# Weight-check loads one output tile earlier, weight casts and copies spread over block 0, in a fused FFN kernel

## The reference, cut to what matters

```
tf    = sigmoid(sum(cond))                          # one number per batch
decay = exp(-exp(w)) * (0.5 + 0.5*tf)
ek, ekv = exp(min(k,30)), exp(min(k,30))*v
nf, df  = forward scans   a = a*decay + ekv (ek)    # along the 1024 steps
nb, db  = the same scans run backward
num = nf + nb - ekv + exp(min(u+k,30))*v            # den likewise
m   = sigmoid(r) * num/max(den,1e-8) * (0.8+0.2*tf)
h   = m @ W1.T            # 1024 -> 4096
q   = clip(round(h/0.1), 16-bit range)
out = x + gelu(q*0.1) @ W2.T                        # 4096 -> 1024
```

## Time and profile before

| | us |
|---|---|
| median of 3 timed runs | 1911.16 (1910.56 to 1913.1) |
| profiled execution, its own time | 1906.45 |
| its span | 1904.6 |
| PE busy | 1723.3 (90%) |
| DVE busy | 1281.7 (67%) |
| ACT busy | 1046.7 (55%) |
| PE waited for `mo` at the starts of blocks (L505) | 59.6 in 7 waits |
| PE waited for the residual addition (L561, L505) | 9.4 + 1.5 |
| block 0's hidden stage, from its third step | 132.25 to 238.6 |

### The profile page before, as it was taken

The page is one execution under the profiler, slowest core; times in us unless marked ns, Lnnn a source line. Parts: engine busy times, 40 slices in busy tenths (PEclk is TensorE's granted clock), DMA queues, the critical chain, the costliest instruction groups (busy, mean ns, idle before and its releaser), DMA issues.

```text
span 1904.6 us, 27493 instructions
## 1 busy us (share of the span) xinstructions
PE 1723.3 (90%) x10882; PEld 1076.1 (57%) x10882; DVE 1281.7 (67%) x2040; ACT 1046.7 (55%) x1422; POOL 24.7 (1%) x44
## 2 busy tenths in 40 slices
PE   1367989899998999899998999989998999989998
PEld 0123434487446864388545874478544884468643
DVE  8964987679586766678685775768776774933211
ACT  5544853488336863388444873378544883345400
POOL 0040000000000000000000000000000000000000
PEclk9678999899998999999998999989998999999999
DMA  8499866465454645456454654556454554545442
GB/s 215 116 238 334 299 204 182 144 198 191 148 168 143 188 150 177 144 181 213 139 174 136 199 170 142 171 169 194 153 183 132 178 189 148 157 132 161 142 146 73
DMA packets 119990, 329.55 MB, mean 173 GB/s; under 512 B 13232, under 2 KB 21424, under 8 KB 119344
## 3 DMA queue, kind: packets, MB, share of 16 engines
q1 hardware_dynamic: 117168, 304.67, 50.5%
q0 software_dynamic: 2688, 23.07, 5.1%
HBM read 319.30 MB, written 48.23 MB: 193 GB/s over the span
## 4 chain that ended last, share of the span: by engine, by line
PE 79%; DMA 3%; DVE 3%; ACT 1%; issue 1%; SPq 0%; DVEq 0%
PE ps L561 42%; PE ps L505 37%; DMA chk_full<-in_w_dram 3%; DVE chk_full L1107 1%; ACT chk_i L758 1%; DVE a L1039 0%; ACT mo L695 0%; DVE a L1041 0%; DVE a L1043 0%; DVE xy L1099 0%; SPq L303 0%; SPq L317 0%; DVE mo L1049 0%; SPq L318 0%; ACT q L699 0%
## 5 line engine op out<-in xcount | busy, mean ns | idle before, releaser
L561 PE MATMUL ps<-act,w_ring 128*128 128x512 f16 x4096 | 890.1, 379 | 9.4 <-DVE xy L1099 9.4
L505 PE MATMUL ps<-mo,w_ring 128*128 128x256 f16 x6272 | 704.4, 276 | 61.2 <-DVE mo L1049 59.6
L505 PEld LDWEIGHTS ps<-mo,w_ring 128*128 128x128 f16 x6272 | 620.5, 99 | 146.7 <-DVE mo L1049 61.6
L561 PEld LDWEIGHTS ps<-act,w_ring 128*128 128x128 f16 x4096 | 400.6, 98 | 490.9 <-issue 15.5
L758 ACT ACTIVATE chk_i<-chk_full 128x1024 int8<-128x1024 f32 x64 | 67.5, 1054 | 440.3 <-DMA chk_full<-in_w_dram 440.3
L1107 DVE SCALAR_TENSOR_TENSOR chk_full<-chk_i,chk_full 128x1024 f32<-128x1024 int8 x64 | 78.3, 1223 | 252.5 <-ACT chk_i L758 252.3
L1092 DVE SCALAR_TENSOR_TENSOR act<-a,act 128x1024 f16<-128x1024 f32 x128 | 156.2, 1220 | 132.3 <-ACT act L751 132.3
L745 ACT ACTIVATE a<-q 128x1024 f32<-128x1024 int16 x128 | 135.3, 1057 | 31.4 <-DVE act L1092 27.2
L751 ACT ACTIVATE act<-a 128x1024 f16<-128x1024 f32 x128 | 134.2, 1049 | 0.9
L482 PE MATMUL ps<-mo,w_ring 128*128 128x512 f16 x128 | 45.1, 532 | 87.3 <-DVE mo L1032 87.3
L495 PE MATMUL ps<-mo,w_ring 128*128 128x512 f16 x384 | 90.0, 399 | 16.5 <-ACT q L699 12.5
(11 more groups left out here) (95 smaller groups left out, 1454.2 us busy)
## 6 DMA issues: line engine op xcount, KB each, us to landing
w_ring<-w1s SPq DMA_DIRECT2D x168, 512.0 KB, 3.7
w_ring<-w_half SPq DMA_DIRECT2D x144, 512.0 KB, 4.2
chk_full<-in_w_dram SPq DMA_DIRECT2D x64, 512.0 KB, 5.2
V<-in_fside_dram SPq DMA_DIRECT2D x64, 256.0 KB, 4.5
R<-in_x_dram SPq DMA_DIRECT2D x64, 256.0 KB, 4.6
w_half<-in_w_dram POOLq DMA_DIRECT2D x16, 1024.0 KB, 14.5
xy<-in_x_dram SPq DMA_DIRECT2D x64, 256.0 KB, 2.6
out_dram<-xy SPq DMA_DIRECT2D x64, 256.0 KB, 4.4
```

The source lines that it names most:

```text
L505: mm = pe.matmul(dst[:, f, :], wp_ring[:, k, r, f, q, :], mo[:, op, q, p, :], start=(fresh and f == 0 and q == 0 and p == 0), stop=(q == K ...
L561: mm = pe.matmul(y_ps[y][:, :], w2_ring[:, k, f, :], act[:, a, p, :], start=(a == 0 and p == 0), stop=(a == FT - 1 and p == 1))
```

## The change

- `load_check` moves forward by one output tile: the load of piece `8n + d + 1` now stands where that of piece `8n + d` stood, and the last of a block stands in the row of tile 6. The second piece's load goes ahead of the ring load for tile 1's second half, and the third piece's load comes right behind that ring load.
- On ACT and DVE each piece's conversion and comparison go behind the work for the next block that followed them (`operands_hi`, `tile_group`, `operand_sums`, `operands_lo`, `part`), and the comparison behind the residual addition, except the first and the last piece's.
- The W2 casts get waits on POOL: on the seventh mixing tile, on block 0's hidden steps and on its first output halves. The copies of W1's quadrants wait for block 0's output halves. SP's ring loads wait for the one cast that they need, and the first of block 1 for the copies, which now have a semaphore each.

No arithmetic is added or taken away.

```diff
                 if i < 2 * STEPS:
                     sp.wait_ge(s_w1cast[i // 2], 16)
-                if i == 2 * STEPS:
-                    for d in range(DT):
-                        sp.wait_ge(s_w2cast[d], 16)
+                if 2 * STEPS <= i < 2 * STEPS + 4:
+                    sp.wait_ge(s_w2cast[i % 2], 16)
+                if 2 * STEPS + 4 <= i < 2 * STEPS + 2 * DT:
+                    sp.wait_ge(s_w2cast[(i - 2 * STEPS) // 2], 16)
...
-                for _ in range(3 if n == 0 else 5):
+                for _ in range(2 if n == 0 else 4):
                     ring_load()
                 load_check(DT * n + 1)
+                ring_load()
+                load_check(DT * n + 2)
                 for d in range(2, DT):
...
-                    load_check(DT * n + d)
+                    if d < DT - 1:
+                        load_check(DT * n + d + 1)
...
             for d in range(DT):
+                if d == 0:
+                    pool.wait_ge(s_out, CT - 1)
+                elif d == 1:
+                    pool.wait_ge(s_h0, 2 * FPS)
+                elif d < 6:
+                    pool.wait_ge(s_h0, FPS * (d + 3))
+                else:
+                    pool.wait_ge(s_y, d - 5)
                 pool.dma_start(w2_half[d], w2_full[d]).then_inc(s_w2cast[d], 16)
             for s in range(STEPS):
+                pool.wait_ge(s_y, 3 + s // 2)
...
@@ DVE, the end of an output stage
-                check(at + 6)
+                check(at + 5)
                 if nxt:
                     operand_sums(n + 1, 2)
                     operands_lo(n + 1, 2)
+                    divide(g0 + 7)
                 residual_sum(n, 6)
-                if nxt:
-                    divide(g0 + 7)
-                check(at + 7)
+                check(at + 6)
                 if nxt:
                     operand_sums(n + 1, 3)
                     operands_lo(n + 1, 3)
+                check(at + 7)
                 residual_sum(n, 7)
```

More of the change, by code:

```diff
@@ L147, in adaln_ffn_kernel @@
         s_w2cast = [sem(f"s_w2cast{k}") for k in range(DT)]
-        s_w1copy = sem("s_w1copy")
+        s_w1copy = [sem(f"s_w1copy{k}") for k in range(STEPS)]
         s_wsumin = [sem(f"s_wsumin{k}") for k in range(2)]
@@ L292, in ring_load @@
                     sp.wait_ge(s_w1cast[i // 2], 16)
-                if i == 2 * STEPS:
-                    for d in range(DT):
-                        sp.wait_ge(s_w2cast[d], 16)
+                if 2 * STEPS <= i < 2 * STEPS + 4:
+                    sp.wait_ge(s_w2cast[i % 2], 16)
+                if 2 * STEPS + 4 <= i < 2 * STEPS + 2 * DT:
+                    sp.wait_ge(s_w2cast[(i - 2 * STEPS) // 2], 16)
                 if i == 2 * STEPS + 2 * DT:
-                    sp.wait_ge(s_w1copy, 16 * 3 * STEPS)
                     for k in range(2):
                         sp.wait_ge(s_wstore[k], 16 * STEPS)
+                    for t in range(STEPS):
+                        sp.wait_ge(s_w1copy[t], 16 * 3)
                 if i >= RING:
@@ L454, in _ @@
             for d in range(DT):
+                if d == 0:
[6 more added lines that the diff above has]
+                    pool.wait_ge(s_y, d - 5)
                 pool.dma_start(w2_half[d], w2_full[d]).then_inc(s_w2cast[d], 16)
             for s in range(STEPS):
+                pool.wait_ge(s_y, 3 + s // 2)
                 pool.wait_ge(s_w1cast[s], 16)
                 for r, h, k in ((WP1, 0, 0), (WP2, 0, 1), (WP4, 1, 1)):
-                    pool.dma_start(w1s[s][:, r, :, :], w1_quads[s][:, h, :, k, :]).then_inc(s_w1copy, 16)
+                    pool.dma_start(w1s[s][:, r, :, :], w1_quads[s][:, h, :, k, :]).then_inc(s_w1copy[s], 16)
             for d in range(DT):
                 pool.wait_ge(s_w2cast[d], 16)
-            pool.wait_ge(s_w1copy, 16 * 3 * STEPS)
+            for s in range(STEPS):
+                pool.wait_ge(s_w1copy[s], 16 * 3)
         @block.tensor
@@ L820, in _ @@
                     hidden_block(n, nxt, g0)
+                if nxt:
+                    operands_hi(n + 1, 0)
                 check_i8(at)
                 if nxt:
-                    operands_hi(n + 1, 0)
+                    tile_group(g0 + 5)
                 check_i8(at + 1)
                 if nxt:
-                    tile_group(g0 + 5)
+                    operands_hi(n + 1, 1)
                 check_i8(at + 2)
                 if nxt:
-                    operands_hi(n + 1, 1)
+                    tile_group(g0 + 6)
                 check_i8(at + 3)
                 if nxt:
-                    tile_group(g0 + 6)
+                    tile_group(g0 + 7)
                 check_i8(at + 4)
-                if nxt:
-                    tile_group(g0 + 7)
                 check_i8(at + 5)
-                check_i8(at + 6)
                 if nxt:
@@ L840, in _ @@
                     reciprocal(g0 + 7)
-                check_i8(at + 7)
+                check_i8(at + 6)
                 if nxt:
                     operands_hi(n + 1, 3)
+                check_i8(at + 7)
             def general_block(m):
@@ L1176, in _ @@
                     hidden_block(n, nxt, g0)
-                check(at)
                 if nxt:
@@ L1180, in _ @@
                     operands_lo(n + 1, 0)
+                check(at)
                 residual_sum(n, 0)
-                check(at + 1)
+                if nxt:
+                    part(3, g0 + 4)
                 residual_sum(n, 1)
                 if nxt:
-                    part(3, g0 + 4)
                     part(0, g0 + 5)
-                check(at + 2)
+                check(at + 1)
                 if nxt:
@@ L1190, in _ @@
                     operands_lo(n + 1, 1)
+                    part(1, g0 + 5)
                 residual_sum(n, 2)
+                check(at + 2)
                 if nxt:
-                    part(1, g0 + 5)
                     part(2, g0 + 5)
                     part(3, g0 + 5)
-                check(at + 3)
                 residual_sum(n, 3)
@@ L1199, in _ @@
                     part(0, g0 + 6)
+                check(at + 3)
+                if nxt:
                     part(1, g0 + 6)
                     part(2, g0 + 6)
-                check(at + 4)
                 residual_sum(n, 4)
@@ L1206, in _ @@
                     part(0, g0 + 7)
+                check(at + 4)
+                if nxt:
                     part(1, g0 + 7)
-                check(at + 5)
                 residual_sum(n, 5)
```

## The result

| | before | after |
|---|---|---|
| median of the timed runs | 1911.55 (1910.56 to 1913.1, 4 runs) | 1857.6 (1856.04 to 1862.72, 4 runs) |
| ratio, with its 95% interval | 1 | 0.9722 (0.9702 to 0.9742) |
| profiled execution, its span | 1906.45, 1904.6 | 1856.92, 1854.3 |
| PE, DVE, ACT busy | 1723.3, 1281.7, 1046.7 | 1710.3, 1282.2, 1044.0 |
| PE's waits at the starts of blocks 1 to 7 | 61.1 | 28.6 |

The change makes the kernel 54 us faster, 2.8%. I had forecast 1810 with a range up to 1838; the time lies 20 us above the range. The direction was right, and half of the gain was missing.

A forecast was written before the change was run, and what follows sets the result against it. PE, busy 90%, was taken as the bound, standing still at block starts and in block 0. 1906.45 - 78.0 - 3.7 - 30.5 + 11.2 = 1805.5; with 4.7 carried over, 1810, range 1796 to 1838.

The forecast's parts named there:

- Starts, the wait removed: Starts of blocks 1 to 7: PE's wait for `mo`, its clock loss and a residual wait go, 78.0 us gained.
- Starts, the new wait: Starts of blocks 1 to 7: PE newly waits 1.6 us each for ACT's `seed`, 11.2 us lost, without clock loss.
- the store takes 4.2 until the next issue: SP's queue at block 2's end: 4.2 us from a store to the next issue, one link of the check's loop.
- My second rival: Block starts: check 6 ends 2 to 4 us later, a longer wait and clock loss add 41 us, 1851; chance 0.12.
- the first three: Cases the range was to hold: the forecast (0.50), no new wait at starts (0.20), part of the wait kept (0.12).
- Waits for the residual in blocks 1 to 7: Output stage outside block 0: PE's waits for the residual go with the late check, 3.7 us gained.
- Block 0: Block 0 from its third hidden step: all waiting and its clock loss go, 30.5 us, 23 of it in the hidden stage.
- nothing in DVE's row is later than PE needs it: End of block 0's hidden stage: DVE needs about 23 us until the first residual addition, PE wants it after 27.7.
- My third rival: Block 0: five casts delay weight-sum loads, so the hidden stage keeps its 23 us, 1833; chance 0.12.
- The offset of 4.7 us: Whole kernel: the timed median lay 4.7 us above the profiled execution, carried over from 1805.5 to 1810.
- The slow rival: Output tiles: SP's loop sets the pace, decisive from about 18.1 us a tile; 1971 at 19.4; chance 0.04.
- The signs that I had named: Profile after: `mo` waits near 0, `seed` waits 1 to 2 us, no clock fall, block 0 in 194 to 198 us.

The follow-up runs named there:

- experiments 5: The changed kernel with two check buffers, the int8 piece placed on a part of `q16`: 1816.63 us, ratio 0.9507.
- 11: The changed kernel with two check buffers, one W2 cast per hidden step, and two pieces of DVE's work in block 0 moved earlier: 1798.98 us, ratio 0.9429.
- Experiment 8: The changed kernel, still one check buffer, with check loads for pieces 3 to 7 issued behind the next tile's store and residual load: 1823.89 us, ratio 0.9552.
- Experiment 4: The changed kernel with each block's last check piece converted behind the next block's second spill and compared behind its second seed: 1857.42 us, ratio 0.9715.
- 9: The changed kernel with two check buffers, but casts and copies as in the kernel before: 1824.75 us, ratio 0.9554.
- experiment 1: The kernel before with only block 0's part of the change (casts and copies spread), the check as before: 1908.4 us, ratio 0.9982.
- experiment 2: The changed kernel with casts and copies as in the kernel before, so the check's part alone: 1862.49 us, ratio 0.9745.

## Why the prediction was right or wrong

*Starts, the wait removed (78.0 us).* Right as a step: the eight microseconds behind the last comparison are gone, and experiments 5 and 11 show runs of 848 matmuls without a gap. What failed is the next term.

*Starts, the new wait (11.2 us).* This term measured 38.1. The mechanism that I gave it is there in the rows, in the order I gave. Four things were off. The first: "the store takes 4.2 until the next issue" is the size that failed: it measured 5.62 to 5.75 at block 2's end and 5.3 to 5.8 over blocks 1 to 6, with the check's load just ahead of the store, where the change itself puts it in time, and I took the price from a place where it wasn't (and from the shortest of six there, 4.2 to 4.6). Experiment 8 moves it away again, and the link is back at 4.4. That is 1.5 us at each start, and my margin on the operand pair was 0.4, so PE waits for `mo` again. The second: "Behind `seed`, DVE's next need is at 807.7 at the earliest and is met" forgot the last residual load, whose addition stands in DVE's row ahead of it and which waits for the store behind the last check load. Experiment 4 shows that mending the forecast wait alone brings nothing. The third: "no clock loss" cost 5.6 us. The fourth: one block's end was taken for all seven, and the addition of tile 6, which has 2.8 us to spare in my working, came late at four of them (6.8 us of the waits).

My second rival, "block starts keep a real part of the wait", is the one that came in kind: check 6 ends 1.4 to 4.2 us later than I had it (it said 2 to 4), and the clock falls at three starts. It had put that down to some tenths on each link, and one link had 1.5 of it. It had 52 us for the starts (the 11.2 and 41 more), so the 38.1 lie between it and the forecast, nearer to it. It had a chance of 0.12 and should have had a far larger one, since the sum stood or fell with a margin of 0.4 us at the end of a chain of some ten links. And the range was set against its own words: it was said to take in "the first three in full", but the second rival's 1851 lies outside its upper end of 1838.

*Waits for the residual in blocks 1 to 7 (3.7 us), and what was costed at nothing.* Right: no wait of PE at L576 is left outside block 0, DVE's and ACT's busy time is the same, and no wait of PE stands behind the copies of W1's quadrants, though beside them a store of SP's took 7.1 us until the next issue (275.63 to 282.75).

*Block 0 (30.5 us).* Its hidden stage is right to the microsecond: 83.04 us for 384 matmuls, as 6 x 13.86. The step that failed is "nothing in DVE's row is later than PE needs it". I had put two sentences side by side that don't go together: five casts in the hidden stage, which leaves three for the output stage, 6.9 us apart; and DVE's budget of "about 23 us until the first residual addition", worked out as if loads came at once. It took 49 us (215.2 to 264.3). "One cast is in flight at a time", at "about 5 us", failed as well: the three took 9.7 to 10.6 us each, so they overlapped. The last weight sums' loads fall right among them. The waits of 12.2 and 8.2 us follow, and some 4.5 of clock. Experiments 5 and 9 between them give the part's value with the loop out of the way, 6.7 us; with the other check (experiment 1) it was 1.9, with the changed kernel's (against experiment 2) 4.9. From experiment 5 to 11 the edits of casts and order give 17.7, so these two together are most of the cause; which has how much of it in that kernel I haven't separated.

My third rival had placed the casts' harm in the hidden stage, where there was none. That its size, 23 us, is close to what the output stage lost is luck. The Trainium skill, DMA: Bandwidth & Descriptors, section "Queues, rings and completion order", has each engine take turns between queues packet by packet; the rows of 225 to 235 us don't show one for one as the earlier trace rows did, since SP's queue moved 1053 packets beside the casts' 67, so they neither bear it out nor refute it. I had used it for that rival only, and not asked which loads a cast would meet in the output stage.

*The offset of 4.7 us* between the profiled and the timed execution did not come back: 1857.6 against 1856.92, 0.7. It was carried over on one pair of numbers, and made the forecast higher, so it didn't cause the miss.

*The slow rival*, SP's loop setting the pace of all tiles, was close in kind. From the comparison's end at 750.5 to the next at 769.2 are 18.7 us, over the 18.1 from which I said that it decides. But the next is 11.1 (769.2 to 780.3), so the loop doesn't go on at that pace, and it costs at the block's end alone.

*The signs that I had named.* V's first load in block 0 landed within 6 us (4.2), and block 0's hidden stage has no wait for the quantisation or the ring. Against it: six of the seven starts wait over 3 us in all, the clock falls at three, and the third hidden step to the end of block 0's outputs took 218.8 us and not 194 to 198.

## What to carry to other kernels

When a wait is moved ahead of other work in an in-order queue, work out what is behind it and put each behind-standing transfer's price at its new place, with the loads that are now issued just ahead of it. Where a second buffer isn't to be had, put the transfer that waits for the slow consumer behind the store and the load that others need: here one moved call got 34 of 41 us. A chain worked out for one block holds for the others only if their rows are the same. Bulk transfers that are spread out must be checked against every step's critical loads up to the last one, not only against the stage that they held up.

## What the runs showed of the hardware

TensorE's clock fell after several short waits, none of them above 2.3 us. Windows of the changed kernel at the start of block 1 (us, busy us and instructions of PE, PEld, DVE, ACT and POOL, granted clock, DMA share, GB/s):

```profile
354.00:356.00 2.00, 0.30 (x3) 0.28 (x4) 1.93 (x5) 0.66 (x1) 0.00 (x0) 1.00 0.73 171
356.00:358.00 2.00, 2.00 (x14) 1.51 (x13) 1.47 (x2) 0.40 (x1) 0.00 (x0) 0.62 0.83 256
358.00:360.00 2.00, 2.00 (x11) 1.44 (x10) 0.60 (x1) 1.54 (x2) 0.00 (x0) 0.52 0.79 313
```

Waits of 1.75 and 1.98 us with six matmuls between them came ahead of it; the clock then stood at its lower level, 1.2 GHz, for three to four microseconds, and cost 1.8 us. In block 4, waits of 1.51, 1.98 and 1.12 us cost nothing (816 matmuls in 89.24 us). In the kernel of experiment 8 a single wait of 2.23 us cost nothing either:

```profile
1191.03 89.24 PE L520 MATMUL ps<-mo,w_ring 128*128 128x256 f16 x816 [2.23 <-ACT ps L720]
```

So the clock's price of a wait isn't read from its own length alone: three of the seven starts paid, and which ones would, these rows didn't tell beforehand. The Trainium skill, TensorE: Matmul & The Clock Gate, section "A second HAM failure mode: psum-queue depth-cycling", tells of one kernel whose PE idles briefly between groups of matmuls, often enough that its clock goes back and forth. The starts of blocks 1, 2 and 3 agree in so far as the clock fell and came back after such short waits; the starts of blocks 4 to 7 had them too, and it didn't fall.

At block 2's end a 256 KB store took 4.4 us from its issue to the next one behind its landing with one 512 KB load of the same queue issued just ahead (experiment 8), and 5.6 to 5.8 with two (the changed kernel).
